# Loading x's third chunk of channels a second time, two tiles side by side, and transposing it with one product

## The reference, cut to what matters

```python
q = heads(x @ W_q); k_t, v_t = heads(text @ W_k), heads(text @ W_v)
probs_t = softmax(q k_t / 4);  text_out = probs_t v_t
sem = l2norm(probs_t text) . l2norm(ip)
probs_ip = softmax(q k_ip / 4 + 0.5 * sem) * spatial_mask;  ip_out = probs_ip v_ip
out = (text_out + ip_out) @ W_out + b_out + x
```

## Time and profile before

| | |
|---|---|
| device time, median of 3 runs | 318.04 us (317.91, 318.04, 320.0) |
| the profiled execution | 319.01 us, its span 317.3 us, mean granted clock 1.0 |
| PE, PEld busy | 301.7 us (95%), 291.1 us (92%) |
| DVE, ACT, POOL busy | 269.5 us (85%), 276.9 us (87%), 210.1 us (66%) |
| DMA | 17.02 MB in 15130 packets, mean 54 GB/s |

### The profile page before, as it was taken

How to read it: one execution, slowest core, us unless ns; L and a number is a source line. 1 busy time by engine, 2 the same in 40 slices (tenths; PEclk the granted TensorE clock), 3 DMA queues, 4 the chain that set the end, 5 groups by cost and what they waited for, 6 DMA issues and landing times.

```text
span 317.3 us, 8813 instructions
## 1 busy us (share of the span) xinstructions
PE 301.7 (95%) x2289; PEld 291.1 (92%) x2289; DVE 269.5 (85%) x1861; ACT 276.9 (87%) x1168; POOL 210.1 (66%) x372
## 2 busy tenths in 40 slices
PE   4899899999999999999999999999999999998976
PEld 3789769888999999999999999999999999998964
DVE  5483846798889898989898989998999899898995
ACT  3744679999999999999999999999999999999942
POOL 3033416687877789688977796889787878675200
PEclk9999999999999999999999999999999999999999
DMA  6980003000120202011110112021202120010011
GB/s 193 347 253 1 0 8 91 2 1 3 32 64 21 66 30 66 25 44 45 30 63 9 56 32 65 22 64 34 64 24 63 34 62 24 23 33 22 24 42 64
DMA packets 15130, 17.02 MB, mean 54 GB/s; under 512 B 2592, under 2 KB 14536, under 8 KB 15080
## 3 DMA queue, kind: packets, MB, share of 16 engines
q1 hardware_dynamic: 15080, 16.44, 17.1%
HBM read 10.55 MB, written 5.24 MB: 50 GB/s over the span
## 4 chain that ended last, share of the span: by engine, by line
PE 79%; DVE 8%; ACT 7%; DMA 2%; POOL 1%; issue 1%; SPq 1%; POOLq 0%
PE gv_ps L1073 23%; PE mi_ps L1108 12%; PE mi_ps L1032 12%; PE sc_ps L1052 10%; PE et_ps L1060 10%; ACT e_sb L619 4%; PE mi_ps L1086 3%; DMA x_nat<-in_x 2%; PE mi_ps L1010 2%; DVE place_ctxT L795 2%; PE gv_ps L1187 2%; PE mi_ps L1012 1%; DVE ktok L847 1%; PE sc_ps L1167 1%; DVE negmax L787 1%
## 5 line engine op out<-in xcount | busy, mean ns | idle before, releaser
L619 ACT ACTIVATE e_sb<-sc_ps,negmax 128x60 f32<-128x60 f32 x640 | 152.6, 353 | 6.3 <-DVE negmax L787 5.1
L795 DVE CUSTOM_DVE_ANT_0 place_ctxT<-gv_ps,e_sb 128x60 f32<-128x60 f32 x640 | 100.8, 213 | 16.9 <-PE gv_ps L1073 15.4
L1073 PE MATMUL gv_ps<-tab,place_w 128*128 128x160 f32 x640 | 113.1, 299 | 0.0
L1073 PEld LDWEIGHTS gv_ps<-tab,place_w 128*128 128x128 f32 x640 | 93.7, 189 | 0.3 <-ACT place_w L637 0.3
L1052 PE MATMUL sc_ps<-km,qs 128*128 128x256 f32 x320 | 77.0, 322 | 0.1
L637 ACT COPY place_w<-et_ps 128x256 f32<-128x256 f32 x160 | 68.5, 428 | 0.2
L1060 PE MATMUL et_ps<-ident,e_sb 128*128 128x128 f32 x320 | 61.9, 275 | 2.9 <-ACT e_sb L619 1.8
L787 DVE TENSOR_REDUCE negmax<-sc_ps 128x4 f32<-128x240 f32 x160 | 63.4, 397 | 0.0
L795 DVE DVE_READ_ACCUMULATOR2_ANT quad<- 128x1 f32 x640 | 52.5, 82 | 0.0
L420 POOL TENSOR_TENSOR km<-ktok,group_mask 128x512 fp32r<-128x512 f32 x40 | 41.3, 1039 | 14.4 <-DVE ktok L847 7.9
L628 ACT COPY fin<-gv_ps 128x80 f32<-128x80 f32 x160 | 43.8, 274 | 6.7 <-DVE quad L795 5.7
(11 more groups left out here) (184 smaller groups left out, 557.2 us busy)
## 6 DMA issues: line engine op xcount, KB each, us to landing
x_nat<-in_x SPq DMA_DIRECT2D x16, 320.0 KB, 3.2
out<-place_w SPq DMA_DIRECT2D x32, 160.0 KB, 1.8
place_ctx<-in_ctx SPq DMA_DIRECT2D x4, 256.0 KB, 3.3
place_w<-in_L_xattn_W_v SPq DMA_DIRECT2D x1, 640.0 KB, 8.0
place_w<-in_L_xattn_W_k SPq DMA_DIRECT2D x1, 640.0 KB, 9.4
place_w<-in_L_xattn_W_k_ip SPq DMA_DIRECT2D x1, 640.0 KB, 11.0
place_w<-in_L_xattn_W_v_ip SPq DMA_DIRECT2D x1, 640.0 KB, 9.5
place_ctxT<-in_L_xattn_W_out SPq DMA_DIRECT2D x1, 640.0 KB
```

Of the source, the lines that this page charges most:

```text
L619: last = nc.scalar.activation(e_sb[:, slot, TOK * j:TOK * j + T], sc_ps[:, bank, TOK * j:TOK * j + T], ACT.Exp, bias=negmax[:, slot, j:j + 1])
L795: last = v.tensor_tensor_reduce(out=junk[:, u % 2, j, 0:T], in0=gv_ps[:, u % 2, TABW * j:TABW * j + T], in1=e_sb[:, u % ERING, TOK * j:TOK ...
L1073: last = mm(gv_ps[:, u % 2, 2 * TABW * r:2 * TABW * r + 2 * TABW], eT[:, u % TRING, P * r:P * r + P], tab[:, b % 2, h:h + 2, :].rearrange( ...
```

## The change

A second tile of x, `x_third`, has two places; each holds the third chunk (64 channels) of both tiles of a half, side by side in 128 columns. SP fills it with a DMA of its own (`load_third`), counted in `in_x3`. That DMA waits until the transposes of the half two before it, which used the same place, are done. Part 1 of `x_transposes` waits for `in_x3` and makes one transpose of the 128 columns, which puts the first tile's chunk on partitions 0 to 63 and the second's on 64 to 127 of PSUM. ACT and DVE take each tile's 64 x 128 by an instruction of its own, two in place of one of 64 x 256.

```diff
+        x_third = sb("x_third", [P, 2, P])
+        in_x3 = [sem(f"in_x3_{n}") for n in range(2)]
...
+            def load_third(half):
+                sp.dma_start(x_third[:, half % 2].rearrange("p (t c) -> p t c", t=2),
+                             x_half(half)[:, :, 2 * P:C]).then_inc(in_x3[half % 2], DMA)
+
             sp.dma_start(x_nat[:, 0], x_half(0)).then_inc(in_x[0], DMA)
+            load_third(0)
             sp.dma_start(wv, w_v.rearrange("(c p) n -> p c n", p=P)).then_inc(in_wv, DMA)
...
             sp.dma_start(mask_sb[:], ip_mask.rearrange("(t p) -> p t", p=P)).then_inc(in_mask, DMA)
+            load_third(1)
             for half in range(1, XRING):
                 sp.dma_start(x_nat[:, half], x_half(half)).then_inc(in_x[half], DMA)
+            for half in (2, 3):
+                sp.wait_ge(xT_done, 2 * half - 2)
+                load_third(half)
...
                 if t % 2 == 1 and half < ALL_HALVES:
                     sp.dma_start(x_nat[:, half % XRING], x_half(half)).then_inc(in_x[half % XRING], DMA)
+                third = t // 2 + 4
+                if t % 2 == 1 and third < ALL_HALVES:
+                    sp.wait_ge(xT_done, 2 * third - 2)
+                    load_third(third)
...
                 else:
-                    nc.scalar.copy(xh[0:64, 2, :], ps[64:P, 0:HALF]).then_inc(xT_hi, 1)
+                    for t in range(2):
+                        last = nc.scalar.copy(xh[0:64, 2, P * t:P * t + P], ps[64 * t:64 * t + 64, 0:P])
+                    last.then_inc(xT_hi, 1)
...
                 else:
-                    v.tensor_tensor(xh[64:P, 2, :], ps[64:P, 0:HALF], xh[0:64, 2, :].bitcast(F32),
-                                    ALU.subtract).then_inc(xT_lo, 1)
+                    for t in range(2):
+                        last = v.tensor_tensor(xh[64:P, 2, P * t:P * t + P], ps[64 * t:64 * t + 64, 0:P],
+                                               xh[0:64, 2, P * t:P * t + P].bitcast(F32), ALU.subtract)
+                    last.then_inc(xT_lo, 1)
...
-                for t in range(2):
-                    if n == 0:
+                if n == 0:
+                    for t in range(2):
                         for c in range(2):
                             last = tr(ps[:, HALF * c + P * t:HALF * c + P * t + P], x_nat[:, slot, t, P * c:P * c + P], ident[:])
-                    else:
-                        last = tr(ps[:, P * t:P * t + P], x_nat[:, slot, t, C - P:C], ident[:])
+                else:
+                    pe.wait_ge(in_x3[half % 2], DMA * (half // 2 + 1))
+                    last = tr(ps[:, 0:P], x_third[:, half % 2], ident[:])
                 last.then_inc(xT_done, 1)
```

## The result

The changed kernel takes 385.69 us (median of 6 runs), the kernel before 318.67 us beside it: 67.0 us more, a ratio of 1.2105 with the 95% interval 1.2069 to 1.2141. The profiled execution took 383.97 us, its span 382.3 us against 317.3, and the mean granted clock fell from 1.0 to 0.924. It is the quickest of the six: the others took 384.97 to 387.62 us, at a mean clock of 0.916 to 0.920.

A forecast was written before the change was run, and what follows sets the result against it. TensorE was taken to set the pace. Waits of 41.0 us, minus 1.7 for the product, plus 0.6 for start, ACT and DVE, plus 14.4 for the clock: 318.04 + 54.3 = 372 us, range 350 to 388.

The forecast's parts named there:

- The place of the wait: Before L1012 in halves 4 to 15: the load is issued in the slot where TensorE wants its data.
- Its size: TensorE's waits for the new load: 11 of 3.54 us and one of 2.1, together 41.0 us.
- The choice to put it behind x: In the DMA queue the new load stays behind x's load, landing at 127.80 us when issued at 124.83.
- The rival in which it passes x: DMA engines take the new load beside x's, so the stall is 2.37 us: 345 us in all, chance 0.12.
- The clock: TensorE's clock falls in three of four stalls, costing 1.6 us each time: 12 x 1.2 = 14.4 us.
- a clock that holds: Rival: TensorE's clock stays up through the stalls, as after the 2.17 us idle time: 358 us, chance 0.20.
- falls in every stall and stays down longer: Rival: TensorE's clock falls at all 12 stalls, losing 2.4 us each: 387 us, chance 0.14.
- The product taken out: One transpose of two goes in each of 16 halves: 16 x 0.107 = 1.7 us off TensorE.
- Whatever delays TensorE is paid in full: Whole run: TensorE, busy 95% of the span, sets the pace, while ACT and DVE have time left.
- ACT and DVE: Their doubled copies and subtractions cost nothing in the 12 stalled halves and 0.3 us together in the other four.
- The cover named there: In stalled halves ACT and DVE catch up while TensorE waits; without that, 12 x 0.3 = 3.6 us.
- The start: Half 0's load, queued between x and W_v, makes the weights behind it land later: 0.3 us, bounds 0 and 1.7.

The follow-up runs named there:

- the load issued first: Changed kernel with the late third-chunk load issued first in the odd tile's round, ahead of the output store and x's load: 338.85 us, ratio 1.0655.
- one product less: Kernel before with the second of L1012's two products left out in halves 4 to 15, copies, subtractions and loads unchanged: 318.82 us, ratio 1.0000.
- the splitting alone: Kernel before with ACT's copy and DVE's subtraction for the third chunk each split into two of 64 x 128, no second load: 319.56 us, ratio 1.0020.
- the earlier load: Changed kernel with the third-chunk load for halves 4 to 15 issued one tile earlier, in the even tile's round: 320.71 us, ratio 1.0067.
- the load alone: Kernel before with the second third-chunk load added at the change's places and used by nobody: 319.25 us, ratio 1.0016.

## Why the prediction was right, and where not

**The place of the wait: right.** The same slot, the same chain, 12 waits, L1033 x16; the store, x and the load are issued in the order and at the distances that the earlier trace rows gave.

**Its size: right.** 41.0 us forecast, 40.4 measured; the load landed 2.80 us after its issue in the half shown, 2.97 forecast. The choice to put it behind x is what the load issued first confirmed (2.0 us without x ahead); that it takes its share by bytes was not tested by itself. The rival in which it passes x was wrong.

**The clock: right in kind, too small.** This is the term that was mis-sized: 12 x 1.2 = 14.4 us forecast, 24.7 behind the waits and 1.7 near the end measured in the profiled execution. I let three of four stalls fall; eleven of twelve did. The pause of 2.17 us that spoke for a clock that holds was a weak witness: the same pause lowered the clock in other kernels here (last section). And I took 1.6 us for a fall from the start of the kernel, where full speed came back after one unbroken stretch of work; here the half clock lasted 3.4 us behind one wait and 6.8 behind the next, in turn, which is 1.7 and 2.9 us of work. The rival "falls in every stall and stays down longer", at 387 us, was the case in all but one wait, and had only 0.14. The Trainium skill ("TensorE: Matmul & The Clock Gate", section "HAM oscillation — how this bites in real kernels") describes a kernel in which a wait of 3 to 5 us for a DMA ends at the half clock at every tile, and this trace agrees in ten of its eleven waits over 3 us; the twelfth, of 2.13 us, ended there too. Of the distance to the forecast, 385.7 - 372 = 13.7 us, 12.0 are this term as the profiled execution has it.

**The product taken out: wrong where it mattered.** 1.7 us were credited for it. Without the waits none of it came (16.49 us a half with one product less, as before); in halves with a wait it is not shown either way. "Whatever delays TensorE is paid in full" is right for a wait of microseconds and wrong for a tenth of one, in both directions. What misled me is that a timeline of TensorE without gaps looks the same with two engines bound as with one: the product starts as soon as the engine is free, and others would have been late just behind.

**ACT and DVE: right for the stalled halves, where they had caught up.** The cover named there was needed: once the waits were gone, the splitting alone cost 0.07 us a half, and the paired form 0.17 although a product was gone, so the earlier load made the kernel slower, 320.71 us, not faster. For this I had a price of 0.3 and no case.

**The start: too dear.** 0.3 us were charged for the weights behind the new load; the run with the load alone shows no cost (x's first load in SP's loop at 91.29 us, 91.39 before).

## What to carry to other kernels

When a change adds a load, ask not how long it takes but what it stands behind in its issuing engine's program, and compare that moment with the slot in which its data are wanted: here the two were the same slot by the kernel's own schedule, and one condition in a loop was worth 65 us. A wait on TensorE can cost more than its length, so a term for the clock belongs beside every stall of some microseconds; filling the wait with throwaway products is a cheap way to measure that term alone. And before crediting work taken off the busiest engine, take away a little of it in an experiment: where engines are balanced to a tenth of a microsecond, as here, removing work from one gained nothing.

## What the runs showed of the hardware that was not expected

The first of the 12 waits, 3.28 us long, left the clock alone, and the other eleven, 2.13 to 3.65 us long, did not. A pause of 2.2 us near the end is in all twelve kernels. In seven profiled executions it left the clock alone, the kernel before among them; in five it did not, the changed kernel, the splitting on both engines and one product less among them. The earlier load is one of the five, as its timeline and a window show:

```profile
309.37 0.52 PE L1107 MATMUL mi_ps<-ident,mixed 128*128 128x128 f32 x3 [2.16 <-DVE mixed L987]
```

```profile
310.00:312.00 2.00, 2.00 (x11) 2.00 (x10) 1.77 (x7) 0.91 (x4) 0.76 (x1) 0.60 0.00 0
```

That is not the earlier load's doing. Of the 23 executions of the kernel before taken beside it, 13 have a mean granted clock of 1.000, eight 0.995 and two 0.989, and those at 0.995 took 1.5 us more in the median (319.03 and 317.52); of its own 12, seven have 0.995. So neither the length of a pause nor the program alone decided whether the clock fell; what else did, no run here isolates. The twelve waits of 1.7 us left it alone in the profiled execution; in the fourth execution of that kernel, at 0.990, no trace shows where it fell.

DVE ran two subtractions on the same 64 partitions closer together (0.50 us the pair) than two on different halves (0.59), and ACT two copies likewise (0.43 and 0.53). Why was not tried.
